# First attention: value matmuls in bursts of three, three and two units instead of pairs, with eight probability slots instead of six

## The reference

```python
# x: (2, 2048, 256), 16 heads of width 16
q, k, v = heads(x @ Wq.T + bq), heads(x @ Wk.T + bk), heads(x @ Wv.T + bv)
scores = einsum('bhqd,bhkd->bhqk', q, k) * hd ** -0.5
decay = exp(-alpha * abs(idx[:, None] - idx[None, :]))
attn = softmax(scores * decay, axis=-1)
out = einsum('bhqk,bhkd->bqhd', attn, v).reshape(B, T, D)
x = layernorm(x + out @ Wo.T + bo)
```

## Time and profile before

| what | value |
|---|---|
| median of 3 runs | 3396.51 us (3393.56 to 3422.1) |
| the profiled execution, its own time | 3414.64 us |
| its span, first to last instruction | 3412.9 us |
| granted TensorE clock, mean over the span | 0.945 |
| PE, DVE, ACT, POOL busy | 91%, 72%, 53%, 41% of the span |
| stretch with the value matmuls of the first attention | 270.5 to 1766 us |

### The profile page before, as it was taken

How to read it: one execution, slowest core, us unless ns; L and a number is a source line. 1 busy time by engine, 2 the same in 40 slices (tenths; PEclk the granted TensorE clock), 3 DMA queues, 4 the chain that set the end, 5 groups by cost and what they waited for, 6 DMA issues and landing times. The chain is left out here.

```text
span 3412.9 us, 66017 instructions
## 1 busy us (share of the span) xinstructions
PE 3093.8 (91%) x22948; PEld 1750.5 (51%) x22949; DVE 2444.9 (72%) x6529; ACT 1802.6 (53%) x2255; POOL 1390.8 (41%) x721
## 2 busy tenths in 40 slices
PE   4679999999999999999967989899999977999996
PEld 2233333333333333333324555566666656999995
DVE  5689999999999999999648888745555554333334
ACT  4227888888888888888863343322222222111112
POOL 3337877878787787877600010000000111111110
PEclk8789999999999999999988999998888998999998
DMA  5863443333333444434121110030000005555555
GB/s 138 214 187 91 92 93 91 82 86 78 79 78 65 92 92 92 88 82 86 35 52 31 25 42 1 1 100 14 14 14 14 19 22 192 185 182 177 181 184 182
DMA packets 201698, 304.65 MB, mean 89 GB/s; under 512 B 86192, under 2 KB 150544, under 8 KB 199248
## 3 DMA queue, kind: packets, MB, share of 16 engines
q1 hardware_dynamic: 192208, 277.73, 31.3%
q0 software_dynamic: 7632, 22.16, 1.9%
q10 hardware_dynamic: 1584, 1.21, 0.1%
HBM read 238.91 MB, written 62.13 MB: 88 GB/s over the span
## 5 line engine op out<-in xcount | busy, mean ns | idle before, releaser
L883 DVE CUSTOM_DVE_ANT_0 ps_r<-ps_r,toep 128x512 f32<-128x512 f32 x1894 | 1253.2, 717 | 71.1 <-PE ps_r L812 31.9
L982 ACT ACTIVATE prob<-ps_s,csc 128x1024 f32<-128x1024 f32 x768 | 830.3, 1117 | 152.1 <-PE ps_s L836 130.0
L940 POOL TENSOR_TENSOR tb<-tb,toep 128x1024 f32<-128x1024 f32 x240 | 568.0, 2367 | 265.8 <-ACT tb L972 227.2
L812 PE MATMUL ps_r<-p 96*128 96x512 bf16 x1894 | 646.8, 383 | 8.9 <-DVE mp L883 4.1
L836 PE MATMUL ps_s<-p 120*128 120x512 bf16 (+1 forms) x2048 | 609.7, 380 | 27.7 <-ACT tb L972 16.4
L943 POOL TENSOR_TENSOR tb<-tb,mb 128x1024 f32<-128x1024 f32 x240 | 567.7, 2366 | 18.8
L852 PE MATMUL ps_o<-prob,vp 128*32 128x256 f32 x8192 | 548.2, 385 | 1.2 <-ACT prob L979 0.9
L812 PEld LDWEIGHTS ps_r<-p 96*128 96x128 bf16 x1894 | 181.5, 96 | 404.7 <-DVE mp L883 257.1
L1708 POOL DMA_INDIRECT slots_scratch<-l_xh,l_place x64 | 62.5, 977 | 726.6 <-DVE l_xh L2033 709.6
L852 PEld LDWEIGHTS ps_o<-prob,vp 128*32 128x32 f32 x8192 | 213.7, 109 | 269.6 <-issue 176.5
L836 PEld LDWEIGHTS ps_s<-p 120*128 120x128 bf16 (+1 forms) x2048 | 189.7, 98 | 238.7 <-ACT tb L972 46.7
(11 more groups left out here) (325 smaller groups left out, 3659.4 us busy)
## 6 DMA issues: line engine op xcount, KB each, us to landing
moe_w<-in_W_dram SPq DMA_DIRECT2D x79, 1024.0 KB, 12.0
p<-scr_scratch SPq DMA_DIRECT2D x288, 192.0 KB
mb<-mrow_scratch SPq DMA_DIRECT2D x16, 2048.0 KB, 8.1
scr_scratch<-part SPq DMA_DIRECT2D x64, 384.0 KB, 7.1
p<-scr_scratch SPq DMA_DIRECT2D x96, 128.0 KB
moe_pt<-slots_scratch SPq DMA_DIRECT2D x72, 132.0 KB, 2.1
vscr_scratch<-vsb SPq DMA_DIRECT2D x8, 1024.0 KB, 10.9
vp<-vscr_scratch SPq DMA_DIRECT2D x16, 512.0 KB, 22.3
```

The lines of the kernel that those rows point to most:

```text
L812: pe.matmul(ps_r[:, bank, :], buf[:, hh, 0, qt * P:(qt + 1) * P], buf[:, hh, 1, kc * CH:(kc + 1) * CH], start=True, stop=True)\
L883: dve.tensor_tensor_reduce(ps_r[:, bank, :], ps_r[:, bank, :], toep[:, col:col + CH], 1.0, -3.0e38, ALU.mult, ALU.max, mp[:, whose.par, hh ...
L940: pool.tensor_tensor(tb[:, k % DIAGS], tb[:, k % DIAGS], toep[:, col:col + CH].unsqueeze(1) .broadcast_to([P, 2, CH]), ALU.mult).then_inc( ...
L982: act.activation(prob[:, n % RING], ps_s[:, mine % 2], ACT.Exp, scale=csc[:, qb * TB + kb:qb * TB + kb + 1]).then_inc(s["exp"], 1)
```

## The change

The values no longer follow in pairs after every second unit. Within 16 units they are issued in bursts of units (0, 1, 2), (3, 4, 5), (6, 7), (8, 9, 10), (11, 12, 13) and (14, 15), each burst behind the score and the small steps of the unit that is 4 later than its last one. Each unit of a burst is a step of its own with its own wait on `exp`. The `prob` ring has 8 slots instead of 6 (2 x 4 KB more in each partition), and the start value of `value` follows it. The sum step stays behind the values that follow the score of the tenth unit of a query block.

```diff
-RING = 6
+RING = 8
 LAG = 4
-EXP0, PV0, EV0 = TB, 5, 1
+BURSTS = ((0, 1, 2), (3, 4, 5), (6, 7), (8, 9, 10), (11, 12, 13), (14, 15))
+EXP0, PV0, EV0 = TB, RING - 1, 1
...
-    for two in range(0, UNITS + (LAG if kind == "last" else 0), 2):
-        for u in (two, two + 1):
-            next_small(EARLY + 2 * u)
-            if u < UNITS:
-                steps.append(("score", u, None, 0))
-            next_small(EARLY + 2 * u + 1)
-        if two >= LAG:
-            steps.append(("values", two - LAG, None, 0))
-        elif kind != "lead":
-            steps.append(("values", UNITS + two - LAG, None, -1))
-        if two % TB == TB // 2 and (two > TB or kind != "lead"):
-            steps.append(("sum", two // TB - 1 if two > TB else QB - 1, slot, 0 if two > TB else -1))
+    for u in range(UNITS + (LAG if kind == "last" else 0)):
+        next_small(EARLY + 2 * u)
+        if u < UNITS:
+            steps.append(("score", u, None, 0))
+        next_small(EARLY + 2 * u + 1)
+        end = u - LAG
+        if end >= 0 or kind != "lead":
+            for burst in BURSTS:
+                if end % TB == burst[-1]:
+                    for n in burst:
+                        steps.append(("values", (end // TB * TB + n) % UNITS, None, 0 if end >= 0 else -1))
+        if u % TB == TB // 2 + 1 and (u > TB or kind != "lead"):
+            steps.append(("sum", u // TB - 1 if u > TB else QB - 1, slot, 0 if u > TB else -1))
             slot += 1
...
-                            pe.wait_ge(s["exp"], up_to(whose.times(UNITS) + n + 2 + EXP0))
-                            for m in (n, n + 1):
-                                qb, kb, _ = e_unit(m)
-                                for f in range(2):
-                                    for hh in range(2):
-                                        q = 2 * f + hh
-                                        out = ps_o[32 * q:32 * q + VW, qb % 2, :]
-                                        mm = pe.matmul(out.rearrange("p (j c) -> p j c", c=P), vp[whose.par][:, kb, hh, :],
-                                                       prob[:, m % RING, hh, :].rearrange("p (j f c) -> p f j c", f=2, c=P)[:, f],
-                                                       start=(m % TB == 0), stop=(m % TB == TB - 1), skip_group_check=True)
-                                mm.then_inc(s["value"], 1)
+                            pe.wait_ge(s["exp"], up_to(whose.times(UNITS) + n + 1 + EXP0))
+                            qb, kb, _ = e_unit(n)
+                            for f in range(2):
+                                for hh in range(2):
+                                    q = 2 * f + hh
+                                    out = ps_o[32 * q:32 * q + VW, qb % 2, :]
+                                    mm = pe.matmul(out.rearrange("p (j c) -> p j c", c=P), vp[whose.par][:, kb, hh, :],
+                                                   prob[:, n % RING, hh, :].rearrange("p (j f c) -> p f j c", f=2, c=P)[:, f],
+                                                   start=(n % TB == 0), stop=(n % TB == TB - 1), skip_group_check=True)
+                            mm.then_inc(s["value"], 1)
```

## The result

The changed kernel is slower: 3454.95 us median of 12 runs against 3397.65 of 12 runs of the kernel before on the same chips, ratio 1.0126, 95% interval 1.0091 to 1.0161. The forecast was 3432.5 in a range of 3408 to 3452, with "slower by over 1%" at 0.5. The sign holds, and so does the size of the ratio (the forecast was 3432.5 / 3396.5 = 1.0106, inside the interval), while the median itself lies 3 us above the range.

What follows compares the result with a forecast made beforehand. PE was taken as the bound, with little room on DVE. Fifteen pairs of heads at +2.20 gave +33.0, units without tiles +3: +36 us on the 3396.5 median, 3432.5 us, range 3408 to 3452.

Steps and rivals of the forecast that it cites:

- burst of three, tile to tile: On PE, from the tile ahead of a three-unit burst to the tile behind it: 1.31 + 2 x 0.215 = 1.74 us.
- tile 4 behind tile 0: Fifth tile of a three-unit stretch: starts at 2.05 us, waiting 0.30 for its bank, instead of 1.745 by PE's order.
- regular stretch of three units: Between first tiles of successive stretches on PE: 4.45 us, against 4.15 by PE's order and 4.26 before.
- stretch behind an evacuation: Three units after ACT copies ps_o: 4.67 us, 0.22 above regular where it was 0.40 before; -0.18 per 16 units.
- stretch where pairs of heads meet: Eight tiles between bursts, the last waiting for tile 4's bank: 5.74 us, 1.29 above regular; +0.11 a pair.
- stretch with the turn step: DVE's short steps delay the second tile, so tile 4 waits to about 2.46: 4.86 us instead of 4.67, +0.19.
- last five query blocks, with the units without tiles: The last 78 units have no tiles: bounds -2.4 (ten bursts saved) and +8.6 (ACT runs dry), middle +3 us.
- The loop of the tiles' banks: Three tile banks between PE and DVE: a tile waits for its bank's drain, making PE wait 0.30 us per long stretch.
- The first rival: PE decides, not the tiles' banks: three of four long stretches 0.30 shorter, -26 us, 3370 us; chance 0.08.
- The waits inside a burst: Each unit's own wait on PE: taken as 0; the rival, broken fetching ahead, +57 us, 3489, chance 0.07.
- the ring of eight: More prob slots for ACT: bounds 0 and -19 us, taken as 0; rival worth 19 us, 3414, chance 0.09.
- a sum step: Tile behind the transposes no longer waits for DVE's last tile after a three-unit burst: -0.21 us, twice a pair.

Runs made afterwards that it cites:

- half2_bursts: The changed kernel with DVE's reduction of every tile cut to 256 of 512 columns; ratio to the kernel before 0.9974, 93.99 us a pair of heads.
- half2_pairs: The kernel before with DVE's reduction of every tile cut to 256 of 512 columns; ratio to the kernel before 0.9957, 93.96 us a pair of heads.
- pairs_ring8: The changed kernel with bursts cut back to two units, keeping eight prob slots and a wait for each unit; ratio to the kernel before 0.9987.
- bursts_ring6: The changed kernel with six prob slots instead of eight; ratio to the kernel before 1.0085.
- singles: The changed kernel with a burst for each unit; one run, 3497.95 us.
- evac_mid: The kernel before with ACT's evacuation moved behind the diagonal score's copy, ahead of the next block's third exponential; ratio to the kernel before 0.9935.

## Why the prediction was right

By its steps, in us, each beside what the timeline of PE after shows:

| step | said | measured |
|---|---|---|
| burst of three, tile to tile | 1.74 | 1.74 |
| tile 4 behind tile 0 | 2.05 | 2.04 |
| regular stretch of three units | 4.45 | 4.45 |
| stretch behind an evacuation | 4.67 | 4.68 |
| stretch where pairs of heads meet | 5.74 | 5.75 |
| stretch with the turn step | 4.86 | 4.87 |
| a pair of heads | 97.2 | 97.17 |
| last five query blocks, with the units without tiles | +3 | +1.5 |
| first attention | +36 | +32.9 |

The evacuation's stretch in the timeline of PE after; it answers to the earlier trace rows:

```profile
1070.67 0.39 PE L814 MATMUL ps_r<-p 96*128 96x512 bf16 x1
...
1072.16 0.61 PE L838 MATMUL ps_s<-p 120*128 120x512 bf16 x2 [0.23 <-ACT tb L973]
...
1073.61 0.38 PE L814 MATMUL ps_r<-p 96*128 96x512 bf16 x1
...
1075.35 0.39 PE L814 MATMUL ps_r<-p 96*128 96x512 bf16 x1
```

Tile 4 isn't late here, the score at 1072.16 was, and the third score comes at 2.49 (1073.16), as said. The last two rows are 1.74 apart, tile to tile over a burst of three. And where pairs meet; it answers to the earlier trace rows. Eight tiles stand between 1038.00 and the next burst, and the row at 1041.35, the last but one of the eight, waits for DVE. For the wait at 1040.05, 2.05 behind the first tile, the profile names ACT; the time is again that at which tile 4 had its bank in the regular stretch:

```profile
1038.00 0.39 PE L814 MATMUL ps_r<-p 96*128 96x512 bf16 x1
...
1040.05 0.39 PE L814 MATMUL ps_r<-p 96*128 96x512 bf16 x1 [0.26 <-ACT prob L983]
...
1041.35 0.39 PE L814 MATMUL ps_r<-p 96*128 96x512 bf16 x1 [0.26 <-DVE mp L884]
...
1043.75 0.39 PE L814 MATMUL ps_r<-p 96*128 96x512 bf16 x1
```

- The loop of the tiles' banks (a tile waits until DVE has read out the one three slots before) held in size and place. That DVE's drain is what makes it is shown by half2_bursts: with a faster drain the 2.1 us a pair become 0.0 (93.99 against 93.96). The other direct test, a fourth bank with the drain as it is, was not run.
- The first rival, that PE's order decides, is out: with the banks as they are by the stretches of 4.45, and it would be out even without the drain's limit, since the scores' banks stand behind it: half2_bursts doesn't beat half2_pairs. Its price of -26 us rested on stretches of 4.15, and the run without the drain's limit has 4.28 and 4.18. I had worked out the third score's wait on ACT only behind an evacuation, and so had not seen that in a regular stretch it would not be ready at 1.96.
- The waits inside a burst and the ring of eight: 0 each, as taken. pairs_ring8 shows both for pairs, bursts_ring6 the ring for bursts; the waits inside a burst of three cost nothing either, since the tiles around it are 1.74 us apart, as worked out without them.
- The term mis-sized most is that of the units without tiles, +3 for the middle of two bounds. The last five query blocks take 94.36 us instead of 92.91 (1704.86 to 1799.22, and 1673.46 to 1766.37 before): +1.5. Two of them cost 0.65 each (39.50 against 38.20), but the very last is 1.55 us shorter.
- The sum +36 is 3 us above the measured 32.9. The first fourteen pairs are 31 us longer together, where 14 x 2.20 = 30.8 was said. From the start of the fifteenth on it is only +2.1 where 2.2 + 3 was said: 1.5 of it in the five query blocks above, and 0.6 in the three ahead of them, at the end of which the tiles stop.
- Three small slips change little. The 0.33 us at the end of a burst isn't in the earlier trace rows; the single records of the trace have it (last group 1020.16, tile 1020.49). For a sum step give 0.51 - 0.27 = 0.24, where 0.21 was taken. And DVE's idle time of 0.6 at a long burst doesn't follow from the 1.9 and 2.32 beside it, whose difference is 0.4; the trace has 0.68.
- A sign that was to show it did not come: PE's busy time in a pair rose by 0.3 us instead of falling, though its idle time grew as said.
- The medians are 57 us apart, 24 more than the attention. Those 24 us are not from the mechanism that was forecast; they go with the granted clock behind the attention. The change by itself is 32.9 of 3397.65 us, 0.97%, just under the 1% of "slower by over 1%", so that the measured ratio lies above 1.01 owes something to luck. Whether the change makes the lower clock more frequent stays open: it is in 7 of 12 runs against 3 of 12, but in 0 of 10 of bursts_ring6, whose attention is as long.

On its edge cost: the Trainium skill's page "TensorEngine Tiling (Array Packing)" states under Key Properties that changing the tiling mode drains the engine. The traces agree in sign, with 0.235 us a burst, and singles pay it at 1.54 us a unit; how much of it is the drain, and how much the change from bf16 to f32, no run separates. That rule alone would have given the wrong sign here. Under PSUM Bottleneck the same page of the Trainium skill states that the emptying of PSUM may become the bound. Here it did, 4.45 us a stretch instead of 4.28, though the banks in question are filled by matmuls that aren't tiled.

## What to carry to other kernels

Merging work of one kind on an engine saves its switching cost, but for that long the engine delivers nothing to the others: compare the longest silence with what the ring between them can hold (here three banks of 0.65 us, 1.95, against 1.74 + 0.58 = 2.32 us; with bursts of two it was 1.31 + 0.58 = 1.89). Work out every ring, not only the tightest, before pricing what its removal would bring. Where the regular period is balanced, look at the exceptions: moving one short copy of ACT behind another one, into a wait that existed anyway, brought 0.65%.

## What was unexpected of the hardware

The granted clock behind the attention differs from one execution of the same program to the next, and how often it is low differs too. The kernel before had a mean clock over the span of 0.945 or less in 5 of 31 executions beside the first experiments, but in 9 of 17 beside evac_mid, on another chip; over its executions the mean goes from 0.939 to 0.955. In the changed kernel some 29 us lie between the two groups (3457.13 against 3428.49, the middle ones of each), about as much as the change itself costs.
